# The gate's two convolutions as bf16 products of three exact parts, 8 columns wide, epsilon on POOL

## What is computed

```python
def _ode_func(A, conv1_w, gn_g, gn_b, conv2_w, conv2_b):
    h = _conv1d(A[:, None, :], conv1_w)          # 1 -> 4 channels, 3 taps
    b, _, n = h.shape
    hg = h.reshape(b, 2, 2, n)
    mu = hg.mean((2, 3), keepdims=True)
    var = hg.var((2, 3), keepdims=True)
    h = ((hg - mu) * lax.rsqrt(var + GN_EPS)).reshape(b, 4, n)
    h = jax.nn.relu(h * gn_g[None, :, None] + gn_b[None, :, None])
    y = _conv1d(h, conv2_w) + conv2_b[None, :, None]   # 4 -> 1, 3 taps
    return y[:, 0, :]
...
attn_base = ((num / (den + 1e-07)) ** 2)[..., 0]   # A, one number per token
A = attn_base + _ode_func(attn_base, ...)
weights = softmax(sigmoid(A), axis=1)
out_low = weights[..., None] * v * ch_w
```

## Time and profile before

| | |
|---|---|
| median of 3 runs | 834.16 us (832.26 to 834.95) |
| the profiled execution's own time | 832.9 us |
| its span | 831.6 us, 18563 instructions |
| PE busy (products / weight loads) | 749.8 us (90%) / 597.5 us (72%) |
| DVE busy | 701.7 us (84%) |
| ACT busy | 662.1 us (80%) |
| POOL busy | 340.9 us (41%) |
| granted TensorE clock, mean | 0.962 of full |
| DMA | 76.50 MB, 92 GB/s |

### The profile page before, as it was taken

The page is one execution under the profiler, slowest core; times in us unless marked ns, Lnnn a source line. Parts: engine busy times, 40 slices in busy tenths (PEclk is TensorE's granted clock), DMA queues, the critical chain, the costliest instruction groups (busy, mean ns, idle before and its releaser), DMA issues.

```text
span 831.6 us, 18563 instructions
## 1 busy us (share of the span) xinstructions
PE 749.8 (90%) x5485; PEld 597.5 (72%) x5485; DVE 701.7 (84%) x2072; ACT 662.1 (80%) x1457; POOL 340.9 (41%) x370
## 2 busy tenths in 40 slices
PE   2789999999999999999999999999675999988872
PEld 1468777787877878888787887887543777777762
DVE  4867877899889889889988988988757799999885
ACT  2456668987997987898799798796744899999994
POOL 3000020133524224243342522337635299886767
PEclk9969999999999999999999999999868999999997
DMA  7113210202222131131213220102114458765430
GB/s 258 27 54 100 76 52 26 84 26 78 71 89 96 53 102 59 55 130 39 78 65 96 90 77 33 51 27 71 58 46 140 122 164 233 211 182 163 148 119 30
DMA packets 50306, 76.50 MB, mean 92 GB/s; under 512 B 8541, under 2 KB 31007, under 8 KB 50208
## 3 DMA queue, kind: packets, MB, share of 16 engines
q1 hardware_dynamic: 39104, 48.42, 20.0%
q0 software_dynamic: 9600, 25.25, 8.4%
q10 hardware_dynamic: 1504, 1.64, 0.6%
HBM read 47.42 MB, written 28.91 MB: 92 GB/s over the span
## 4 chain that ended last, share of the span: by engine, by line
PE 63%; ACT 16%; issue 9%; DVE 5%; POOL 4%; ACTq 1%; DMA 0%; DVEq 0%; POOLq 0%; SPq 0%
PE bank L592 8%; ACT G_S L1904 6%; PE bank L799 6%; PE bank L812 6%; PE bank L672 4%; ACT G_y L1920 3%; PE bank L544 3%; PE bank L674 3%; PE bank L673 3%; PE bank L684 3%; PE bank L620 2%; PE bank L621 2%; ACT G_T L1880 2%; PE bank L604 2%; PE bank L767 2%
## 5 line engine op out<-in xcount | busy, mean ns | idle before, releaser
L3462 POOL TENSOR_TENSOR R<-rstd,mhalf 128x4 f32<-128x4 f32 x16 | 19.5, 1220 | 278.8 <-DVE rstd L1961 278.8
L3633 POOL DMA_INDIRECT out<-G_y,Gid x72 | 83.6, 1161 | 35.4 <-ACT G_y L1920 13.2
L1904 ACT ACTIVATE G_S<-bank,e1b,e1s 128x256 f32<-128x256 f32 (+1 forms) x188 | 95.1, 651 | 2.2 <-PE bank L1285 2.2
L1285 PE MATMUL bank<-G_T,E1T 128*128 128x256 f16 (+1 forms) x752 | 76.4, 251 | 8.0 <-issue 4.4
L592 PE MATMUL bank<-X,PT 128*128 128x257 f32 x320 | 81.0, 392 | 1.1 <-DVE X L2005 0.9
L3506 POOL DMA_INDIRECT rrec<-R,pos x64 | 67.0, 1047 | 29.2 <-issue 20.7
L3497 POOL DMA_INDIRECT hrec<-HN,pos x64 | 65.7, 1027 | 29.0 <-issue 16.0
L1297 PE MATMUL bank<-E2T,G_Sh 128*128 x288 | 65.6, 274 | 9.5 <-DVE G_Sl L3437 9.2
L1285 PEld LDWEIGHTS bank<-G_T,E1T 128*128 x752 | 59.7, 99 | 19.6 <-issue 11.6
L812 PE MATMUL bank<-E2T,Sh 128*128 128x256 f16 x256 | 60.8, 282 | 6.3 <-DVE Sl L2138 6.3
L1297 PE MATMUL bank<-E2T,G_Sl 128*128 x288 | 65.8, 275 | 0.0
(11 more groups left out here) (392 smaller groups left out, 2459.2 us busy)
## 6 DMA issues: line engine op xcount, KB each, us to landing
XT<-in_xT SPq DMA_DIRECT2D x16, 512.0 KB, 3.9
X<-in_x SPq DMA_DIRECT2D x16, 512.0 KB, 5.8
G_h<-hrec SPq DMA_DIRECT2D x25, 257.0 KB, 3.6
G_r<-rrec SPq DMA_DIRECT2D x25, 257.0 KB, 3.5
e1n<-in_ew SPq DMA_DIRECT2D x8, 512.0 KB
e2n<-in_ew SPq DMA_DIRECT2D x8, 512.0 KB, 3.4
G_h<-hrec SPq DMA_DIRECT2D x22, 128.5 KB, 2.1
G_r<-rrec SPq DMA_DIRECT2D x22, 128.5 KB, 2.3
```

Source lines behind the costliest of these rows:

```text
L1285: last = pe.matmul(bk[:, o + a:o + b], E1T[:, e, c, ff * P:(ff + 1) * P], gt[:, x, c, a:b], start=k == 0, stop=k == 3)
L1904: last = act.activation(G_S[w % NGS][:, ff, a:b], bk[:, o + a:o + b], ACT.Silu, bias=e1b[:, e, ff], scale=e1s[:, e, ff])
L3633: pool.indirect_dma_start(t["out"], bass.IndirectOffsetOnAxis(Gid[w % NGI][:, j:j + 1], 0), G_y[w % NGY][:, j, :], None, bounds_check=TOK ...
```

## The change

The 0/1 matrices become bf16. A is no longer copied for the four channels but kept with 8 columns (2 batches x 4 tiles), and split into three bf16 parts that add up to it exactly (o_Ap: the value rounded, the rest rounded, and the rest of that). Each of the five f32 products of `nb` becomes three bf16 products of 8 (or, across the border, 6) columns, and the multiplication by taps reads the 24 columns of PSUM repeated over the channels. The three taps o_t of the second convolution are split in the same way (o_tp, four new steps of 24 columns) for `nb2`. The product that added epsilon in `gn2` goes; POOL adds it before its power, with a wait on a new semaphore between. The gate has 34 steps now. In the loop, `nb` moves behind `nmrow` and `up(.., 2)`, and `nb2` behind `x2T(2g, 1)`. In the setup a memset of epsx becomes a second one of onesN.

```diff
-    from_prev = sb("from_prev", [P, P])
-    from_next = sb("from_next", [P, P])
-    edge_prev = sb("edge_prev", [P, P])
-    edge_next = sb("edge_next", [P, P])
+    from_prev = sb("from_prev", [P, P], BF16)
+    from_next = sb("from_next", [P, P], BF16)
+    edge_prev = sb("edge_prev", [P, P], BF16)
+    edge_next = sb("edge_next", [P, P], BF16)
...
-    o_A = sb("o_A", [P, GB, CH, NT])
+    o_A = sb("o_A", [P, GB, NT])
+    o_Ap = sb("o_Ap", [P, 3, GB, NT], BF16)
+    o_tp = sb("o_tp", [P, 3, TAPS, GB, NT], BF16)
+    o_d = sb("o_d", [P, TAPS, GB, NT])
...
-    epsx = sb("epsx", [P, GB * CH * NT])
...
-    NO = 27
+    NO = 34
...
+        taps = [banks[2][:, k * GC:(k + 1) * GC].rearrange("p (b j) -> p b j", b=GB) for k in range(TAPS)]
 
         def nb(g):
             if not 0 <= g < B // GB:
                 return
-            pe.wait_ge(s["ode"], NO * g + 8)
+            pe.wait_ge(s["ode"], NO * g + 11)
...
-            pe.matmul(taps[0], from_prev[:], A_tok, start=True, stop=False)
-            pe.matmul(taps[0][:, :, 1:NT], edge_prev[:], A_tok[:, :, 0:NT - 1], start=False, stop=True)
-            pe.matmul(taps[1], ident[:], A_tok, start=True, stop=True)
-            pe.matmul(taps[2], from_next[:], A_tok, start=True, stop=False)
-            pe.matmul(taps[2][:, :, 0:NT - 1], edge_next[:], A_tok[:, :, 1:NT], start=False, stop=True).then_inc(s["nb"], 1)
+            for k in range(3):
+                pe.matmul(taps[0], from_prev[:], o_Ap[:, k], start=k == 0, stop=False)
+            for k in range(3):
+                pe.matmul(taps[0][:, :, 1:NT], edge_prev[:], o_Ap[:, k, :, 0:NT - 1], start=False, stop=k == 2)
+            for k in range(3):
+                pe.matmul(taps[1], identb[:], o_Ap[:, k], start=k == 0, stop=k == 2)
+            for k in range(3):
+                pe.matmul(taps[2], from_next[:], o_Ap[:, k], start=k == 0, stop=False)
+            for k in range(3):
+                last = pe.matmul(taps[2][:, :, 0:NT - 1], edge_next[:], o_Ap[:, k, :, 1:NT], start=False, stop=k == 2)
+            last.then_inc(s["nb"], 1)
...
-            pe.wait_ge(s["ode"], NO * g + 13)
-            pe.matmul(banks[2][:, 0:GW], onesN[:], epsx[:], start=True, stop=False)
-            pe.matmul(banks[2][:, 0:GW], onesN[:], sq_flat, start=False, stop=True).then_inc(s["gn2"], 1)
+            pe.wait_ge(s["ode"], NO * g + 16)
+            pe.matmul(banks[2][:, 0:GW], onesN[:], sq_flat, start=True, stop=True).then_inc(s["gn2"], 1)
...
-            pe.wait_ge(s["ode"], NO * g + 20)
-            pe.matmul(out2, from_prev[:], o_t[:, 0], start=True, stop=False)
-            pe.matmul(out2[:, :, 1:NT], edge_prev[:], o_t[:, 0][:, :, 0:NT - 1], start=False, stop=False)
-            pe.matmul(out2, ident[:], o_t[:, 1], start=False, stop=False)
-            pe.matmul(out2, from_next[:], o_t[:, 2], start=False, stop=False)
-            pe.matmul(out2[:, :, 0:NT - 1], edge_next[:], o_t[:, 2][:, :, 1:NT], start=False, stop=True).then_inc(s["nb2"], 1)
+            pe.wait_ge(s["ode"], NO * g + 27)
+            for k in range(3):
+                pe.matmul(out2, from_prev[:], o_tp[:, k, 0], start=k == 0, stop=False)
+            for k in range(3):
+                pe.matmul(out2[:, :, 1:NT], edge_prev[:], o_tp[:, k, 0, :, 0:NT - 1], start=False, stop=False)
+            for k in range(3):
+                pe.matmul(out2, identb[:], o_tp[:, k, 1], start=False, stop=False)
+            for k in range(3):
+                pe.matmul(out2, from_next[:], o_tp[:, k, 2], start=False, stop=False)
+            for k in range(3):
+                last = pe.matmul(out2[:, :, 0:NT - 1], edge_next[:], o_tp[:, k, 2, :, 1:NT], start=False, stop=k == 2)
+            last.then_inc(s["nb2"], 1)
...
             fuse(2 * g - 1)
-            nb(g - 1)
             nmrow(2 * g + 1)
             up(2 * g - 3, 2)
+            nb(g - 1)
             up(2 * g - 3, 3)
             gn1(g - 1)
...
             pv(2 * g + 1, 0)
             pv(2 * g + 1, 1)
-            nb2(g - 1)
             if g == 0:
                 map_et1(1)
                 map_dg(1)
             x2T(2 * g, 1)
+            nb2(g - 1)
             pv(2 * g + 1, 2)
             if g == 0:
...
-                a = o_nd[:, 0].rearrange("p (b j) -> p b j", b=GB)[:, :, None, :].to_broadcast([P, GB, CH, NT])
-                ins = dve.tensor_tensor(o_A[:], a, a, ALU.mult)
+                a = o_nd[:, 0].rearrange("p (b j) -> p b j", b=GB)
+                dve.tensor_tensor(o_A[:], a, a, ALU.mult)
+                ins = dve.tensor_tensor(o_Ap[:, 0], a, a, ALU.mult)
             elif k == 8:
+                ins = dve.tensor_tensor(o_d[:, 0], o_A[:], o_Ap[:, 0], ALU.subtract)
+            elif k == 9:
+                ins = dve.tensor_copy(o_Ap[:, 1], o_d[:, 0])
+            elif k == 10:
+                ins = dve.tensor_tensor(o_Ap[:, 2], o_d[:, 0], o_Ap[:, 1], ALU.subtract)
+            elif k == 11:
                 dve.wait_ge(s["nb"], g + 1)
-                ins = dve.tensor_tensor(o_T[:].rearrange("p t b c j -> p (t b c j)"), bk[:, 0:TAPS * GW],
-                                        W1x[:].rearrange("p t b c j -> p (t b c j)"), ALU.mult)
-            elif k == 9:
+                a = bk[:, 0:TAPS * GC].rearrange("p (n j) -> p n j", j=NT)[:, :, None, :].to_broadcast([P, TAPS * GB, CH, NT])
+                ins = dve.tensor_tensor(o_T[:].rearrange("p t b c j -> p (t b) c j"), a, W1x[:].rearrange("p t b c j -> p (t b) c j"), ALU.mult)
...
+                ins = dve.tensor_copy(o_tp[:, 0], o_t[:])
+            elif k == 24:
+                ins = dve.tensor_tensor(o_d[:], o_t[:], o_tp[:, 0], ALU.subtract)
+            elif k == 25:
+                ins = dve.tensor_copy(o_tp[:, 1], o_d[:])
+            elif k == 26:
+                ins = dve.tensor_tensor(o_tp[:, 2], o_d[:], o_tp[:, 1], ALU.subtract)
+            elif k == 27:
                 dve.wait_ge(s["nb2"], g + 1)
-                ins = dve.scalar_tensor_tensor(o_e[:], bk[:, 0:GC].rearrange("p (b j) -> p b j", b=GB), c2b[:], A_one, ALU.add, ALU.add)
-            elif k == 21:
+                ins = dve.scalar_tensor_tensor(o_e[:], bk[:, 0:GC].rearrange("p (b j) -> p b j", b=GB), c2b[:], o_A[:], ALU.add, ALU.add)
...
             ode(g - 1, 7)
             max_(2 * g + 1, 3)
+            ode(g - 1, 8)
             ve1(2 * g)
+            ode(g - 1, 9)
+            ode(g - 1, 10)
             Sl_(2 * g - 3, 0)
             if g == 9:
                 sort(4)
-            ode(g - 1, 8)
+            ode(g - 1, 11)
             if g == 0:
...
             rinv(2 * g + 1, 0)
-            ode(g - 1, 19)
+            ode(g - 1, 22)
             TTl_(2 * g, 0)
+            ode(g - 1, 23)
+            ode(g - 1, 24)
+            ode(g - 1, 25)
+            ode(g - 1, 26)
             x1(2 * g + 1, 0)
...
-            pool.wait_ge(s["ode"], NO * g + 14)
+            pool.wait_ge(s["ode"], NO * g + 17)
+            pool.tensor_scalar(o_rs[:], o_rs[:], 1e-5, None, ALU.add).then_inc(s["gnv"], 1)
+            pool.wait_ge(s["gnv"], g + 1)
             pool.tensor_tensor(o_rs[:], o_rs[:], mhalf[:, 0:2 * GB], ALU.pow).then_inc(s["gnr"], 1)
```

More of the change, by code:

```diff
@@ L2763, in dve_program @@
         x2(2, 1)
-        for i in range(8, 11):
+        for i in range(11, 14):
             ode(0, i)
         ve1(2)
-        for i in range(11, 14):
+        for i in range(14, 17):
             ode(0, i)
```

136 lines of the change are left out of this document (72 added, 64 removed), and 2 rows, old and new, of the table names.

## The result

| | before | after |
|---|---|---|
| median of 4 runs each | 834.08 us (832.26 to 834.95) | 848.08 us (847.53 to 849.02) |
| ratio, 95% interval | | 1.0173 (1.0158 to 1.0188) |
| profiled execution: time, span | 832.9, 831.6 us | 849.02, 847.4 us |
| mean granted clock | 0.962 | 0.954 |

The change makes the kernel 1.7% slower, 14 us where the prediction had 6 to 7: the direction was right, the forecast size was half of the measured one, and 848.08 lies outside the range (833 to 845).

What follows compares the result with a forecast made beforehand. PE was taken as the engine without a pause, with DVE just behind it. 1.1 us more in each of six periods (+6.6) and 0.3 in gates 0 and 7 each gave +7.2 us, 840.5 us, range 833 to 845.

Steps and rivals of the forecast that it cites:

- step 4: POOL before o_h: adding epsilon costs 0.29 us (0.1 to 0.5) ahead of a 1.41 us power; o_h 1.03 us later.
- Step 6: PE at the gate's end: a 1 us pause before x2T, and pv's third tile 1.1 us later, PE's savings included.
- the rest of the walk: Gate 2 followed in program order over DVE, PE and POOL: 1.1 us more per period, POOL's part included.
- fifteen products in 0.47 us: PE, each convolution: fifteen bf16 products take 0.47 us in place of 1.03, so 0.56 us less.
- o_T 2.8 us after o_A: Sign on DVE around the first convolution: this distance at 2.8 us and not 2.1.
- the four o_tp steps between TTl and x1: DVE before x1: four steps of 24 columns add 0.70 us (bounds 0.4 and 0.9).
- x1 12.3 us after o_A: Sign on DVE late in the gate: x1 starts 12.3 us after o_A, where it was 10.5.
- Step 3: DVE up to the variance: no pause absorbs the delay, o_sq ends 0.74 us later, the variance product starts at 247.30.
- Step 2: PE's order: the first convolution behind nmrow and up(.,2) makes o_T start 0.74 us later, although the convolution is shorter.
- PE's saving: Rival, PE through the periods: DVE has more slack, 1.3 us per gate are gained, 823 us; chance 0.10 with partial cases.
- The bf16 products at their load's pace: Rival, PE's convolutions: fifteen loads of 96 ns make each 1.44 us, +18 us, 851 in all; chance 0.04.
- the 81 ns: Skill's pace per weight load and matmul pair: fifteen cost 1.2 us, total near 849; shares the load-pace rival's chance, 0.04.

Runs made afterwards that it cites:

- e6_pool_warm: The changed kernel with the same addition on a scratch tile put ahead of POOL's wait for o_rs: 851.0 us, ratio 1.0191 to the kernel before.
- e8: The changed kernel with DVE's 1.22 us sum with pb_row moved behind the normalizing step in the loop: 848.25 us, ratio 1.0163 to the kernel before.
- e1: The changed kernel with epsilon added by PE's own product again and no addition on POOL: 838.71 us, ratio 1.0046 to the kernel before.
- e2: The kernel before with only POOL's addition of epsilon in place of PE's epsilon product: 847.34 us, ratio 1.0151 to the kernel before.
- e9: The changed kernel with 26 unused bf16 products in PE's pause ahead of the second x2T of gates 1 to 6: 849.74 us, ratio 1.0209.
- e5: The changed kernel with the first convolution moved back ahead of nmrow in the loop: 850.68 us, ratio 1.0206 to the kernel before.
- v1: The changed kernel with the first convolution back ahead of nmrow, the second in f32, epsilon as one bf16 product on PE: 836.82 us, ratio 1.0026.
- v2: The v1 kernel with the second convolution's four f32 matrices set up on POOL behind all other setup: 834.59 us, ratio 1.0014 to the kernel before.

## Why the prediction was wrong

**Failed: step 4, POOL.** It priced the addition with its handoff at 0.29 us, with a bound of 0.5, from a tensor_scalar of the setup at 0.20 that ran while DVE stood still. Alone it is indeed 0.22 (e6_pool_warm, gate 7). Beside the two DVE steps it is 1.73, and o_rs to o_h grew by 1.40. The sign stood in the rows of the kernel before: the power took 1.41 us in the earlier trace rows, and I read that as its price. In gate 7 of the same kernel it takes 1.04, and in gate 2 this copy ran beside it (POOL at gate 7, DVE at gate 2, before):

```profile
582.85 1.04 POOL L3478 TENSOR_TENSOR o_rs<-o_rs,mhalf 128x4 f32<-128x4 f32 x1 [0.77 <-DVE o_rs L2221]
```

```profile
247.41 0.68 DVE L2388 TENSOR_SCALAR ev<-e1n 128x1024 f16<-128x1024 f32 x1
```

So 0.37 was a wait for the copy (the same 0.37 by which the addition in e8 exceeds its 0.22), and the 1.22 us step did not hold the power off as well. An instruction inserted ahead of it loses that place: the addition runs at the end of the 1.22 us step, and the power, that "hid under" this step, comes behind it. e1 and e2 give the term in periods: 1.4 and 1.3 us, against 0.3.

**Missing: the granted clock.** Step 6 foresaw a pause of 1 us before x2T; it is 1.84 to 2.02 us, and behind it the clock fell in two periods, some 1.5 us each. No term and no bound had that. With POOL's addition gone (e1) or the pause filled (e9) it did not fall. The kernel before has the pattern once, in gate 0: PE stands still for 1.98 us up to 125.99, and its stage table then reads

```profile
124.00:126.00 2.00, 0.02 (x2) 0.04 (x1) 1.95 (x4) 2.00 (x6) 0.00 (x0) 1.00 0.11 40
126.00:126.40 0.40, 0.40 (x4) 0.40 (x5) 0.40 (x1) 0.40 (x2) 0.00 (x0) 0.93 0.00 0
126.40:129.70 3.30, 3.30 (x12) 2.72 (x11) 2.47 (x7) 2.55 (x5) 0.00 (x0) 0.50 0.00 0
```

**Right: the rest of the walk.** The forecast without POOL's part is some 0.8 us per period; e1 has 0.7. In parts (forecast, then measured): fifteen products in 0.47 us, 0.38; o_T 2.8 us after o_A, 2.65 (245.47 to 248.12), against 2.08 before; the four o_tp steps between TTl and x1 0.70 us, 0.74 (258.08 to 258.82); x1 12.3 us after o_A, 13.35, and step 4's error is that 1.1. Two smaller errors cancel by luck. Step 3 was too dear: o_A to o_rs grew by 0.4 (6.45 to 6.86) and not by 0.74. From o_h to x1 it grew by 1.0 (2.24 to 3.25) and not by the 0.70 of the four steps. Step 2 put o_T's delay (0.74; measured 0.57) down to nb's new place, and e5 bears it out: with nb back ahead of nmrow the period falls by 0.6.

**Gates.** Of the 16.5 us between gate 0 and gate 7, 4.6 are the rest of the walk (e1), 3.1 the two dips, and the remaining 8.9 POOL's addition. The forecast, for all eight gates, had 4.9, 0 and 2.3.

**The rivals.** PE's saving did not arrive: no period fell below 69.5 in any version. The bf16 products at their load's pace fell with 0.025 us each; by that row also the 81 ns that the prediction cited from the Trainium skill (TensorE: Matmul & The Clock Gate, Part 2, Back-to-back issue gap) did not come at 8 columns. The 849 that the prediction worked out from it lies close to the measured 848 by coincidence: the products cost less than forecast, and the loss is POOL's and the clock's.

## What to carry to other kernels

Before giving POOL a small step, look at what DVE does in the same microseconds: the price is the time to the end of DVE's run of copies at double rate and of steps with two SBUF inputs, and cutting those up does not help. A DVE step with one operand in PSUM cost POOL nothing here. When a POOL row beside such work is longer than the same row elsewhere, the difference is already a wait, and the next instruction placed ahead of it may miss its slot. A pause of 1.2 to 2 us on PE can cost more than itself, since the clock may fall behind it.

## What the runs showed of the hardware

- A POOL addition of 128x4: 0.22 us alone (e6, gate 7) and beside a 0.68 us DVE step with one operand in PSUM (e2, gate 7), 0.59 beside DVE's 0.68 us copy, 1.73 beside the copy and the 1.22 us addition, 1.93 with the latter in four. The power of 128x4: 1.04 alone, 1.41 beside the copy, 2.55 in gate 4 of v1 and v2.
- Bf16 products of 8 and 6 columns with new weights for each: 0.025 us from start to start.
- Open: why the power gets in between copy and addition and POOL's own addition does not; why the clock falls behind some pauses of 1.2 to 2.1 us only (15 of 48); and what moves the time outside the gates by some 5 us between kernels.
